# Projecting V as three rounded passes over 128 tokens, moved to its two halves by VectorE alone

## The reference

```
proj = xn @ in_proj_w + in_proj_b              # 768 columns: V, control 0, control 1
v = proj[..., :256]
for i in range(2):
    h = implicit_filter(2048, ...)             # one filter of 2048 steps for each channel
    v = causal_convolution(v, h)
    xc = conv3(control_i) + conv_b[i]          # three taps
    v = v * (xc * sigmoid(xc @ gate_w[i] + gate_b[i]))
attention = v @ out_proj_w + out_proj_b
ffn = two products with ternary weights, a squared relu between them, and a rank-16 branch
```

## Time and profile before

| | us |
|---|---|
| median of 3 runs | 860.69 (860.06 to 862.17) |
| the profiled execution | 857.83 |
| its span in the profile | 856.0 |
| busy: PE 830.3, DVE 617.5, ACT 471.6, POOL 201.0 | share of the span 97%, 72%, 55%, 23% |

### The profile page before, as it was taken

The page is one execution under the profiler, slowest core; times in us unless marked ns, Lnnn a source line. Parts: engine busy times, 40 slices in busy tenths (PEclk is TensorE's granted clock), DMA queues, the critical chain, the costliest instruction groups (busy, mean ns, idle before and its releaser), DMA issues.

```text
span 856.0 us, 25946 instructions
## 1 busy us (share of the span) xinstructions
PE 830.3 (97%) x9920; PEld 693.7 (81%) x9921; DVE 617.5 (72%) x1054; ACT 471.6 (55%) x701; POOL 201.0 (23%) x235
## 2 busy tenths in 40 slices
PE   8799999999999998999999999999999999999997
PEld 3588887888888867788888888888888888888997
DVE  7988899889988884555655565556646666567887
ACT  6967777777777854454444444444444444443221
POOL 4944566456645301010101010000000000000000
PEclk9999999999999999999999999999999999999999
DMA  8853432342233278768777868778887877951895
GB/s 224 247 218 115 160 120 98 116 161 115 98 120 140 92 188 227 157 152 194 173 169 154 202 150 202 145 181 182 192 149 182 181 183 132 219 109 49 226 321 195
DMA packets 90544, 142.03 MB, mean 166 GB/s; under 512 B 12846, under 2 KB 70591, under 8 KB 89471
## 3 DMA queue, kind: packets, MB, share of 16 engines
q1 hardware_dynamic: 72846, 101.80, 49.9%
q0 software_dynamic: 7728, 28.05, 10.2%
q10 hardware_dynamic: 9920, 11.54, 4.1%
HBM read 97.39 MB, written 43.97 MB: 165 GB/s over the span
## 4 chain that ended last, share of the span: by engine, by line
PE 51%; DVE 5%; issue 3%; DMA 1%; DVEq 0%; SPq 0%
PE pp L1401 14%; PE py L1420 14%; PE pf L1370 12%; PE pf L1376 3%; PE py L1457 2%; PE py L1388 2%; DVE pp L1169 2%; DMA lead<-filters 1%; DVE GC L1179 1%; DVE xb L1179 1%; PE pp L465 1%; PE pp L467 1%; PE pp L466 1%; PE pf L465 1%; PE pf L467 1%
## 5 line engine op out<-in xcount | busy, mean ns | idle before, releaser
L1300 ACT ACTIVATE r<-pf,fscale 128x512 f32<-128x512 f32 x128 | 88.0, 688 | 124.2 <-PE pf L1376 124.0
L1420 PEld LDWEIGHTS py<-vwin,lead 64*64 64x64 f32 x5120 | 132.7, 132 | 26.8 <-issue 26.8
L1420 PE MATMUL py<-vwin,lead 64*64 64x128 f32 (+4 forms) x5120 | 146.9, 265 | 2.2 <-issue 1.3
L1305 ACT ACTIVATE r_hi<-r 128x512 fp32r<-128x512 f32 x128 | 80.8, 632 | 122.9 <-DVE r L1184 122.9
L1370 PE MATMUL pf<-tokens,split_a 128*128 (+1 forms) x512 | 139.4, 394 | 0.4 <-issue 0.4
L1401 PE MATMUL pp<-wproj,r_hi 128*128 128x256 f32 x512 | 134.6, 296 | 3.8 <-DVE GC L1179 1.8
L1189 DVE TENSOR_TENSOR r_lo<-r,r_hi 128x512 fp32r<-128x512 f32 x128 | 88.2, 689 | 67.2 <-ACT r_hi L1305 67.1
L1401 PE MATMUL pp<-wproj,r_lo 128*128 128x256 f32 x512 | 126.8, 281 | 0.0
L506 POOL TENSOR_SCALAR lead<-lead,norms 128x256 f32<-128x256 f32 x64 | 118.0, 1854 | 3.8 <-POOL norms L500 3.4
L674 DVE SCALAR_TENSOR_TENSOR xc<-ctrl,taps,xc 128x512 f32<-128x512 f32 x128 | 97.7, 783 | 18.5 <-ACT xc L781 17.7
L1401 PEld LDWEIGHTS pp<-wproj,r_hi 128*128 128x128 f32 x512 | 96.2, 188 | 18.3 <-issue 7.4
(11 more groups left out here) (190 smaller groups left out, 1504.9 us busy)
## 6 DMA issues: line engine op xcount, KB each, us to landing
lead<-filters SPq DMA_DIRECT2D x128, 320.0 KB, 6.3
xnT_hbm<-split_b SPq DMA_DIRECT2D x32, 512.0 KB, 3.3
tokens<-xnT_hbm POOLq DMA_DIRECT2D x30, 512.0 KB, 4.9
lead<-in_attn_x SPq DMA_DIRECT2D x16, 512.0 KB, 4.0
gc_hbm<-xc SPq DMA_DIRECT2D x16, 512.0 KB, 2.6
GC<-gc_hbm SPq DMA_DIRECT2D x32, 256.0 KB, 6.6
out<-GC ACTq DMA_DIRECT2D x15, 512.0 KB, 7.2
GC<-in_attn_x POOLq DMA_DIRECT2D x9, 512.0 KB, 7.6
```

The costliest lines, as they stand in the source:

```text
L1300: act.activation(r[j][:, :], pf[:, j, :], ACT.Relu, scale=fscale[:, m:m + 1]).then_inc(relu_done, 1)
L1305: act.activation(r_hi[j][:, :], r[j][:, :], ACT.Copy).then_inc(r_hi_done, 1)
L1420: last = pe.matmul(py[g % 2][q * BW:(q + 1) * BW, side, l, :, A:NB], tile[rows, q * PAIR + l, j * BW:(j + 1) * BW], vwin[g % 2][rows, q, l ...
```

## The change

V is computed by `split_mm`, from the high and low parts that the controls use already: the stationary operand is 128 tokens, the moving one all 256 channels of `in_proj_w`'s V part, itself split once into `Wvs` at the start. The PSUM tile then has 128 tokens on 128 partitions (two blocks of 64, `parity`) and all channels along the row. The wanted layout has the side on the partition half instead, so VectorE moves the result in four additions, each of 64 partitions by 128 channels by 4 blocks; two of the four read one half of the partitions and write the other, and each writes every second block. V's bias is added in the same four instructions.

`xnT` and its copy on ScalarE are gone. `next_low` reads the PSUM tile itself. Chunk 0 gets its parts in the buffers `xcs[1]` instead of `xn`, a plain copy of it, `x0_rows`, stays in the setup stage, and the weights `ranks` are kept elsewhere until stored. The transpositions ahead wait for `xn_split` instead of the two copies. The early loads of the next stage wait for V of chunk 15 (`v_mm`) instead of its controls.

```diff
@@ project_stage, step -1: the split of V's weights, on ScalarE and VectorE @@
+                    for k in range(KT):
+                        act.activation(Wvs_sides[0][:, k], Wv_sides[:, k], ACT.Copy).then_inc(wv_ready, 1)
...
+                    dve.wait_ge(wv_ready, 1 + KT)
+                    for k in range(KT):
+                        last = dve.tensor_tensor(Wvs_sides[1][:, k], Wv_sides[:, k], Wvs_sides[0][:, k].bitcast(F32), ALU.subtract)
+                    last.then_inc(wv_ready, 1)
@@ project_stage, SyncE, last front step @@
-                    sp.wait_ge(ctrl_mm, 4 * NCH)
+                    sp.wait_ge(v_mm, NCH)
@@ project_stage, VectorE: next_low and the move of V @@
-                    if s0:
-                        dve.wait_ge(xnT_done, s + 2)
-                    dve.tensor_tensor(xn[1][:, :, :], xnT[:, :, :] if s0 else pT[:, :, :], xn[0][:, :, :].bitcast(F32), ALU.subtract).then_inc(xn_split, 1)
+                    dve.tensor_tensor(xn[1][:, :, :], pT[:, :, :], xn[0][:, :, :].bitcast(F32), ALU.subtract).then_inc(xn_split, 1)
...
-                    dve.tensor_tensor(V[:, :, bass.ds(batch(dve, s, s0), 1), TB * k:TB * k + TB].rearrange("p c n a -> p c (n a)"),
-                                      pn[:, :, :].rearrange("p i c -> p c i"),
-                                      bv_row[:, :].unsqueeze(2).broadcast_to([P, SLOTS_V, TB]), ALU.add).then_inc(v_stored, 1)
+                    for parity in range(SIDES):
+                        rows = slice(parity * BW, (parity + 1) * BW)
+                        for side in range(SIDES):
+                            channels_of = slice(side * BW, (side + 1) * BW)
+                            last = dve.tensor_tensor(V[channels_of, :, bass.ds(batch(dve, s, s0), 1), TB * k + parity:TB * k + TB:SIDES].rearrange("p c n a -> p c (n a)"),
+                                                     pn_tiles[rows, :, side * SLOTS_V:(side + 1) * SLOTS_V].rearrange("p t c -> p c t"),
+                                                     bv_row[channels_of, :].unsqueeze(2).broadcast_to([BW, SLOTS_V, TT]), ALU.add)
+                    last.then_inc(v_stored, 1)
@@ project_stage, ScalarE @@
-                def next_rows():
-                    act.wait_ge(v_mm, s + 1)
-                    act.wait_ge(xn_split, s + 1)
-                    act.activation(xnT[:, :, :], pT[:, :, :], ACT.Copy).then_inc(xnT_done, 1)
...
                 if ahead:
                     act.wait_ge(xT_mm, s + 2)
-                    if s0:
-                        next_rows()
-                    act.wait_ge(xn_split, s + 1)
                     act.wait_ge(xn_saved[0], 16 * s + 16)
                     act.activation(xn[0][:, :, :], pT[:, :, :], ACT.Copy).then_inc(xn_hi_done, 1)
@@ project_stage, TensorE @@
                 def next_transposed():
                     pe.wait_ge(xn_ready, s + 2)
-                    pe.wait_ge(xnT_done, s + 1)
-                    pe.wait_ge(xn_hi_done, s + 1)
+                    pe.wait_ge(xn_split, s + 1)
...
-                    pe.wait_ge(xnT_done, s + 1)
-                    for i in range(TB):
+                    if s0 == 0:
+                        pe.wait_ge(wv_ready, 2 + KT)
+                    for i in range(TT):
...
-                        ts = slice(i * BW, (i + 1) * BW)
+                        ts = slice(i * P, (i + 1) * P)
                         for k in range(KT):
-                            for side in range(SIDES):
-                                last = pe.matmul(pn[side * BW:(side + 1) * BW, i, :].rearrange("p (h c) -> p h c", h=KT),
-                                                 xnT[:, k, ts], Wv_sides[:, k, :, side, :], start=(k == 0), stop=(k == KT - 1))
+                            last = split_mm(pe, pn_tiles[:, i, :], (x_hi[:, k, ts], x_lo[:, k, ts]),
+                                            (Wvs[:, 0, k, :], Wvs[:, 1, k, :]), k == 0, k == KT - 1)
                     last.then_inc(v_mm, 1)
```

More of the change, by code:

```diff
@@ L50, with setup_stage @@
 HALF = PARTS * RANK
-def setup_stage(nc, hbm, ident, bv_row, flag, V, GC1, Wv, Win, Wgate, eps, half, load_x, load_taps, norm, norms, tern, ranks, fscale, stored, weights_stored, xn, xnT, x0, xn_ready, first_done):
+def setup_stage(nc, hbm, ident, bv_row, flag, V, GC1, Wv, Win, Wgate, eps, half, load_x, load_taps, norm, norms, tern, fscale, stored, weights_stored, xn, x0, xn_ready, first_done):
     (in_w, in_b, out_b, freqs, w1, b1, w2, b2, w3, b3, decay, gate_w, fast_b, w_fc, w_proj, u, v, gate,
@@ L324, in _ @@
             dve.wait_ge(xn_hi_done, 1)
-            dve.wait_ge(xnT_done, 1)
-            dve.tensor_tensor(xn[1][:, :, :], xnT[:, :, :], xn[0][:, :, :].bitcast(F32), ALU.subtract).then_inc(xn_split, 1)
+            dve.wait_ge(x0_copied, 1)
+            dve.tensor_tensor(xn[1], x0_rows[:, :, :], xn[0].bitcast(F32), ALU.subtract).then_inc(xn_split, 1)
             dve.wait_ge(srow_mm, 1)
@@ L369, in _ @@
             act.wait_ge(xT_mm, 1)
-            act.activation(xn[0][:, :, :], x0T, ACT.Copy).then_inc(xn_hi_done, 1)
-            act.activation(xnT[:, :, :], x0T, ACT.Copy).then_inc(xnT_done, 1)
+            act.activation(xn[0], x0T, ACT.Copy).then_inc(xn_hi_done, 1)
+            act.activation(x0_rows[:, :, :], x0T, ACT.Copy).then_inc(x0_copied, 1)
             act.wait_ge(ternT_mm, 1)
@@ L515, in x_tile, with project_stage @@
     return x.rearrange("n (q i p) d -> (n q) p i d", i=TT, p=P)[bass.ds(c, 1)].rearrange("c p i d -> (c p) i d")
-def project_stage(nc, x, xnT_hbm, gc2_hbm, ident, bv_row, V, GC1, Wv, Win, Wgate, eps, xt, x_loaded, xn_ready, norm, taps, bias_in, gc2_saved, xn, xcs, load_ahead, stored, weights_stored, store_weights, xnT, peaks, flag, first_done, tail):
+def project_stage(nc, x, xnT_hbm, gc2_hbm, ident, bv_row, V, GC1, Wv, Win, Wgate, eps, xt, x_loaded, xn_ready, norm, taps, bias_in, gc2_saved, xn, xcs, load_ahead, stored, weights_stored, store_weights, Wvs, peaks, flag, first_done, tail):
     with ExitStack() as ctx:
@@ L573, in project_stage, with split_rows @@
         batch_of = {}
+        Wv_sides = Wv[:, :, :].rearrange("p k (h s c) -> p k h s c", h=KT, s=SIDES)
+        Wvs_sides = [Wvs[:, part, :, :].rearrange("p k (s h c) -> p k h s c", s=SIDES, h=KT) for part in range(2)]
+        pn_tiles = pn[:, :, :].rearrange("p (t u) c -> p t (u c)", u=SIDES)
+        def split_rows(s0):
+            return xcs[ORDERS - 1] if s0 == 0 else [part[:, :, :] for part in xn]
         def batch(eng, s, s0):
@@ L612, in step @@
                         sp.dma_start(xnT_hbm[part, bass.ds(s + 1, 1)].rearrange("c p k t -> (c p) k t"),
-                                     xn[part][:, :, :].bitcast(F32)).then_inc(xn_saved[part], 16)
+                                     split_rows(s0 + 1)[part].bitcast(F32)).then_inc(xn_saved[part], 16)
                 if s0 == NCH - 1:
                     sp.wait_ge(xT_mm, NCH)
-                    sp.wait_ge(ctrl_mm, 4 * NCH)
+                    sp.wait_ge(v_mm, NCH)
                     for part in range(2):
@@ L920, in step @@
                     for _ in range(7):
-                        pe.matmul(pT[:, 0, :], ident[:, :], xnT[:, 0, :], start=True, stop=True)
+                        pe.matmul(pT[:, 0, :], ident[:, :], Wvs[:, 0, :, :].bitcast(F32).rearrange("p k c -> p (k c)"), start=True, stop=True)
                 if back:
@@ L1588, in load_taps @@
                     sp.dma_start(taps[:, cs, 5], gate_b[o, :].rearrange("(c p) -> p c", p=P)).then_inc(bias_in, 16)
-            first_done = [weights.enter_context(nc.semaphore(n)) for n in ("xT_mm", "xn_hi_done", "xnT_done", "xn_split")]
-            xnT = weights.enter_context(nc.sbuf_tensor("xnT", [P, KT, CH], F32))
+            first_done = [weights.enter_context(nc.semaphore(n)) for n in ("xT_mm", "xn_hi_done", "wv_ready", "xn_split")]
+            Wvs = weights.enter_context(nc.sbuf_tensor("wv_split", [P, 2, KT, D], F32R))
             peaks = weights.enter_context(nc.sbuf_tensor("peaks", [P, 2, 4], F32))
```

24 lines of the change are left out of this document (11 added, 13 removed).

## The result

The changed kernel takes 879.57 us (median of 4 runs) against 860.38 us for the kernel before (median of 4 on the same chip): a ratio of 1.0205, with a 95% interval of 1.018 to 1.0229. It is slower, and 3.1 us slower than predicted. The profiled execution took 878.94 us with a span of 877.2 us; 873.6 and 871.8 were forecast.

The account below looks back on a forecast made before the run. VectorE's own list was taken to bound project_stage's steps, GpSimd's loop close behind. The longer move of V adds 15.8 us to the profiled 857.83, giving 873.6; with 2.9 us to the median, 876.5 us, range 869 to 882.

Parts of the forecast that it names:

- The bound, and the steps: In project_stage: VectorE's list, with 0.61 us slack before next_low, sets the pace; steps grow from 17.07 to 18.1 us.
- V's products and the copy, at nothing: TensorE's V group saves 0.6 us, ScalarE's dropped copy shortens GpSimd's loop by 0.93 us to 16.14; neither shortens the step.
- The price of the move: VectorE's four additions of V take 2.73 us without overlap against 1.13 before, adding 1.60 us a step.
- The lower end of the bound: VectorE's four additions of V with 0.08 us overlap between neighbours: 2.41 us.
- the upper end: VectorE's four additions with a 0.06 us pause behind each: 2.97 us a move, 880.4 us in all; chance 0.12.
- The sum: Along VectorE's list: step 0 +1.0, steps 1 to 13 +12.7, step 14 +0.9, step 15 +1.2, together 15.8 us.
- The last stage as long as before: The mix stage behind project_stage keeps its length; its early loads, issued at most 3.47 us later, cost nothing.
- The total: Whole kernel: 873.6 us against the profiled execution, plus 2.9 us to the median of the runs, gives 876.5 us.
- The clock: TensorE's clock stays at its upper level, 2.4 GHz, although its waits grow in each step.
- Overlap: V's four additions on VectorE overlap like neighbours on the same partitions, 2.41 us a move; 871.4 us; chance 0.22.
- two halves side by side: V's additions on different halves run two at once, 1.37 us; the step follows GpSimd's loop; 848.6 us; chance 0.05.
- Double price for strided writes: Writing every second block of V halves each addition's rate, 4.85 us a move; 910.5 us; chance 0.04.

Follow-up runs that it names:

- The run with a move of 1.13 us: The changed kernel with V moved by the earlier single 128 x 1024 addition on VectorE, V's layout wrong: 857.08 us, ratio 0.9959.
- the best of these kernels: The changed kernel with three of V's four pieces moved by ScalarE, one copied by VectorE, bias added on TensorE: 859.35 us, ratio 0.9970.
- the two copies: The changed kernel with two of V's pieces on ScalarE, two as plain VectorE copies, bias added on TensorE: 859.16 us, ratio 0.9981.

## Why the prediction was right, and where its sizes were off

*The bound, and the steps.* Right. The step went by VectorE's list: 18.14 us (18.1 forecast), no idle time before `next_low`, taps' waits unchanged. The kernel before with four additions, within 0.02 us a step of the changed one and at the same time (877.87 us; 879.57 and 877.91), shows that nothing else of the change counts for the steps while the long move stands.

*V's products and the copy, at nothing.* Right while the long move stands. The 24 products of V start between 130.9 and 133.7 us (2.85 us forecast for the group), and the 0.6 us turned into the 0.99 us before `gates(0)`.

*The price of the move.* The mechanism was right, for the reason given: neighbours on different halves do not overlap. The lower end of the bound was met by a run, 2.39 us on one half (2.41 forecast); on alternate halves the move takes 2.82 us, above the value taken (2.73) and below the upper end (2.97). The size rested on a single small row at the program's start, so that it came this close was in part luck. The missing 0.09 us a move is the main error in the sum; each addition is followed by about 0.02 us and not by nothing, and not by the 0.06 us of the earlier trace rows. The Trainium skill's rule (VectorE: DVE Perf Modes, section on two Vector instructions with no wait between them) agrees with both kernels: 0.60 us from start to start where the partitions stay, 0.70 us where they change.

*The sum.* 17.7 us for 15.8: step 0 gave 1.15 for 1.0, steps 1 to 13 gave 13.55 for 12.7 (13 × 0.09 = 1.2 for the move, less some tenths that I can't place), step 14 gave 1.14 for 0.9. Steps 15 and 16 gave 1.88 for 1.2, and a part of that is a wait that I did not see: in step 16 ScalarE's tap 0 of the third tile waits until a store of `xc` has left the buffer that it writes. The store is not issued later beside the step's taps (324.51, the first tap at 325.32; 307.99 and 308.30 before), but it takes 5.2 us from issue to landing where the median of the 16 such stores is 2.6. The kernel before with four additions, whose early loads are those of the kernel before, has 0.27 us there, released by VectorE; so the wait does not come with the long move, and what else of the change makes the store slow is not shown.

```profile
329.73 0.81 ACT L796 ACTIVATE xc<-ctrl,taps 128x512 f32<-128x512 f32 x1 [1.31 <-DMA gc_hbm<-xc]
```

*The last stage as long as before.* Wrong by 3.5 us in the profile that was compared, 2.7 in the second (535.3 against 532.6). The place is the wait for a filter and the low clock behind it; the cause of the wait is open.

*The total.* Against the profiled execution the forecast was short by 878.94 - 873.6 = 5.3 us: 1.9 in the steps and 3.5 in the last stage. The median was missed by 3.1 us only because I added 2.9 us, the distance of the old kernel's median from its profiled execution, and in the changed kernel this distance is 0.6 us. That part is luck.

*The clock.* I said that it stays up. Mostly so, but not behind the filter wait above (0.50 for 5 us), and in step 1 TensorE waited 2.89 us and the granted clock of that stretch was 0.91:

```profile
60.00:80.00 20.00, 17.45 (x88) 14.65 (x88) 18.70 (x40) 14.04 (x21) 8.36 (x10) 0.91 0.29 106
...
62.21 0.19 PEld L467 LDWEIGHTS pc<-tokens,wgate_hi 128*128 128x128 f32 x1 [2.89 <-issue]
```

The wait of 2.89 us alone does not bring the dip: the second profile of the changed kernel has the same 2.89 us at 63.92 and a clock of 1.00 from 60 to 80 us. Other executions show the same dip at 20 to 40 or 40 to 60 us, the kernel before with four additions among them, and even the first profile of the kernel before has 0.91 from 840 us on, which the digit 9 of the earlier trace rows hides; where the last stage starts, they differ by up to 1.9 us for the same code (323.13 and 325.02 for the kernel before).

*The rivals.* Overlap (871.4) is what the additions would do on one half: 870.15 us measured there, in one run. The 848.6 us of two halves side by side did not come, and its price was wrong by my own terms: with a move of 1.37 us VectorE's list is 17.07 - 0.61 + 0.24 = 16.70 us, longer than the loop of 16.14, so at most 0.37 us a step could be gained, not 0.93. The run with a move of 1.13 us bears this out: the rest of the change gives 3.6 us and not 12, with steps of 16.79 us. Double price for strided writes: none.

## What to carry to other kernels

Before an instruction is cut into pieces, read what its partitions do: half the partitions at the same number of elements take the same time, so four half pieces cost twice the whole, and alternating between halves adds another 0.1 us each on top. A gain on one engine counts only up to the next bound: here 0.9 us off one loop was worth 0.3 us, since the second list stood at most 0.6 us behind it. If such a move has to stay, put the pieces and the bias where other engines are idle; but count those engines' next bounds as well. In the best of these kernels that won back the loss and 0.3% more.

## What was not expected of the hardware

Additions of 64 x 512 start 0.60 us apart on the same partitions and 0.70 us apart when either the half that is read or the half that is written changes. A change of the one read is enough, as the additions in another order show, where it alone changes twice, and so is a change of the one written, as the two copies show. The pause that this leaves, 0.02 us behind each, is a third of the one at the program's start.
